# A vision tower on one core: gelu rows weighted before the projection, attention rows divided before P·V, merged products, a new beginning and orders written out

## What is computed

```
h = h + attn0(layernorm(h))     # 16 heads, rope, causal softmax, Wo
h = h + moe(layernorm(h))       # 8 experts, top-2 gates, linear in/out
h = h + attn1(layernorm(h))     # scores, 8 mixed value groups, Wf, relu block
h = h + ffn1(layernorm(h))      # the last stage

def ffn1(x):                    # absmean() makes weights -1, 0 or 1
    h = x @ absmean(W_fc).T     # 256 -> 1024
    h = gelu(h)
    h = (h - mean(h)) * rsqrt(var(h) + eps) * ln_w + ln_b
    return h @ absmean(W_proj).T    # 1024 -> 256
```

## Time and profile before

| | us |
|---|---|
| median of three runs | 561.5 |
| the profiled execution | 560.32 |
| its span | 558.5 |
| TensorE busy | 506.9 (91%) |
| VectorE busy | 375.7 (67%) |
| ScalarE busy | 272.9 (49%) |
| GpSimd busy | 190.3 (34%) |

### The profile page before, as it was taken

One profiled execution on the slowest core, in us unless ns is written; L12 is line 12 of the kernel. 1 busy time (PEld: TensorE's weight loads), 2 busy tenths in 40 slices (PEclk: granted clock), 3 DMA queues, 4 the chain that ended last, 5 costly groups with the idle time before them and its releaser, 6 DMA issues.

```text
span 558.5 us, 12004 instructions
## 1 busy us (share of the span) xinstructions
PE 506.9 (91%) x3850; PEld 424.5 (76%) x3850; DVE 375.7 (67%) x943; ACT 272.9 (49%) x634; POOL 190.3 (34%) x257
## 2 busy tenths in 40 slices
PE   2969999999999887789999999999999989889996
PEld 2758878878787665567778888888888778668885
DVE  4554464555466667565997878878878787648874
ACT  3021213232331363547668777777777886434332
POOL 3320321322323311375463364364363311222230
PEclk9788899999999999999999999999999999979999
DMA  8741333243140500000000000000000000000000
GB/s 318 285 175 38 141 150 120 80 175 150 31 169 0 179 2 2 0 1 2 1 1 2 2 0 0 0 0 0 0 0 0 2 0 1 2 9 21 21 18 22
DMA packets 8685, 29.60 MB, mean 53 GB/s; under 512 B 1936, under 2 KB 3152, under 8 KB 6352
## 3 DMA queue, kind: packets, MB, share of 16 engines
q1 hardware_dynamic: 8656, 29.23, 14.4%
HBM read 27.98 MB, written 1.25 MB: 52 GB/s over the span
## 4 chain that ended last, share of the span: by engine, by line
PE 42%; DVE 5%; issue 5%; ACT 3%; POOL 1%; DVEq 1%; POOLq 0%; ACTq 0%
PE score L2051 6%; PE tb L1803 3%; PE score L1868 3%; PE bz L2081 3%; PE tb L1805 3%; PE tb L1804 3%; PE bank L1805 3%; PE bank L1804 3%; PE bank L1803 3%; PE tb L1886 2%; PE bz L2063 2%; PE bz L1817 2%; PE bz L1803 1%; DVE we_h L1433 1%; PE tb L1817 1%
## 5 line engine op out<-in xcount | busy, mean ns | idle before, releaser
L378 POOL TENSOR_TENSOR h<-h,scaled 114x256 f32 (+1 forms) x88 | 69.0, 784 | 49.3 <-ACT scaled L681 42.7
L330 POOL TENSOR_TENSOR small<-small,half 114x1 f32<-114x1 f32 x44 | 25.7, 584 | 139.4 <-DVE small L964 139.3
L547 ACT ACTIVATE p_exp<-sc,cst 114x608 f32<-114x608 f32 x66 | 48.1, 794 | 24.7 <-DVE sc L1045 24.7
L1915 PE MATMUL bz<-ebuf 128*128 128x256 f32 x256 | 58.9, 383 | 0.0
L1915 PEld LDWEIGHTS bz<-ebuf 128*128 128x128 f32 x256 | 47.8, 192 | 6.0 <-issue 0.2
L1886 PE MATMUL tb<-cst,p_exp 114*114 114x114 f32 x352 | 44.0, 266 | 9.0 <-ACT p_exp L547 3.4
L555 ACT ACTIVATE pt<-tb 114x456 f32<-114x456 f32 x66 | 34.6, 556 | 35.3 <-PE tb L1886 35.3
L2051 PE MATMUL score<-v,pt 114*114 114x137 f32 x352 | 48.9, 282 | 0.3 <-ACT o L648 0.3
L1886 PEld LDWEIGHTS tb<-cst,p_exp 114*114 114x114 f32 x352 | 35.2, 134 | 18.2 <-ACT pt L555 6.7
L681 ACT ACTIVATE scaled<-bank,gl 114x256 f32<-114x256 f32 x88 | 39.0, 473 | 17.3 <-DVE gl L1249 5.9
L2051 PEld LDWEIGHTS score<-v,pt 114*114 114x114 f32 x352 | 44.1, 178 | 2.1 <-issue 0.4
(11 more groups left out here) (216 smaller groups left out, 1338.7 us busy)
## 6 DMA issues: line engine op xcount, KB each, us to landing
ebuf<-in_w_in SPq DMA_DIRECT2D x8, 1024.0 KB, 4.8
ebuf<-in_w_out SPq DMA_DIRECT2D x8, 1024.0 KB, 6.8
x_raw<-in_x_tiles SPq DMA_DIRECT2D x11, 342.0 KB, 3.0
out<-h SPq DMA_DIRECT2D x10, 114.0 KB
raw<-in_w_a SPq DMA_DIRECT2D x4, 256.0 KB, 4.2
ebuf<-in_fc SPq DMA_DIRECT2D x1, 1024.0 KB, 5.6
ebuf<-in_proj SPq DMA_DIRECT2D x1, 1024.0 KB, 7.6
raw<-in_w_a SPq DMA_DIRECT2D x2, 384.0 KB, 5.2
```

What stands on the lines that cost most here:

```text
L378: gp.tensor_tensor(h[0:R, t, :], h[0:R, t, :], scaled[0:R, e % 4, :], ALU.add).then_inc(moe_acc, 1)
L547: act.activation(p_exp[0:R, :, b * S:(b + 1) * S], sc[0:R], ACT.Exp, bias=cst[0:R, CB + b:CB + b + 1], scale=SCALE).then_inc(exps, 1)
L1915: last = pe.matmul(bz[:, m * D:(m + 1) * D], ebuf[:, 0, c * D + m * P:c * D + (m + 1) * P], ebuf[:, 1, c * D:(c + 1) * D], start=(c == 0), ...
```

## The change

**Last stage.** The projection now takes the ternary weights as they are, so two terms suffice. The gelu rows are centred and multiplied by `ln_w` before they are transposed: columns 0 to 511 by GpSimd in two instructions, columns 512 to 1023 by VectorE in one. `proj_hi`, `proj_lo`, `lnw_halves`, `lnw_low`, `proj_sums`, `keep_sums` and `d2_centre` go. The gelu output has two buffers.

```diff
+            def d2_weigh(t):                       # GpSimd
+                gp.wait_ge(g_stat, 4 * t + 4)
+                since(gp, gT_mm, 2 * t)
+                gp.tensor_tensor(gel_w[0:R, 0:512], gel[t % 2][0:R, 0:512], gst[0:R, t, 0:1].broadcast_to([R, 512]),
+                                 ALU.subtract).then_inc(gel_even, 1)
+                gp.wait_ge(gel_even, 2 * t + 1)
+                gp.tensor_tensor(gel_w[0:R, 0:512], gel_w[0:R, 0:512], lnw_row[0:R, 0:512], ALU.mult).then_inc(gel_even, 1)
...
+            def d2_weigh(t):                       # VectorE
+                dve.wait_ge(g_stat, 4 * t + 4)
+                since(dve, gT_mm, 2 * t)
+                V.scalar_tensor_tensor(gel_w[0:R, 512:HID], gel[t % 2][0:R, 512:HID], gst[0:R, t, 0:1], lnw_row[0:R, 512:HID],
+                                       ALU.subtract, ALU.mult).then_inc(gel_odd, 1)
...
             def d2_out(t):
-                V.scalar_tensor_tensor(h[0:R, t, :], x1[0:R], gst[0:R, t, 2:3], h[0:R, t, :],
+                V.scalar_tensor_tensor(h[0:R, t, :], tb[0][0:R, 0:D], gst[0:R, t, 2:3], h[0:R, t, :],
                                        ALU.mult, ALU.add).then_inc(done, 1)
...
             def d2_proj(t):
                 for c in range(HC):
-                    last = mm3(tb[0][0:R, 0:D], gth[:, c, :], gtl[:, c, :], pw_h[c], pw_l[:, c, :], c == 0, c == HC - 1)
+                    pe.matmul(tb[0][0:R, 0:D], gth[:, c, :], projt[:, c, :], start=(c == 0), stop=False)
+                    last = pe.matmul(tb[0][0:R, 0:D], gtl[:, c, :], projt[:, c, :], start=False, stop=(c == HC - 1))
```

**Rows divided.** In the first attention one exponential makes the 608 dense columns, VectorE sums, inverts and multiplies the rows, and three copies scaled by 0 or 1 spread them over the images. The ones products and the division after P·V go; `a2_o` and `a2_lo` read PSUM.

```diff
+            def a2_exp(n):                          # ScalarE
+                act.wait_ge(shifted, 2 * n + 2)
+                act.activation(sc[0:R], sc[0:R], ACT.Exp, scale=SCALE).then_inc(dense, 1)
+
+            def a2_wide(n, batches=range(G)):
+                act.wait_ge(scaled_rows, n + 1)
+                since(act, pt_mm, 4 * n)
+                for b in batches:
+                    act.activation(p_exp[0:R, :, b * S:(b + 1) * S], sc[0:R], ACT.Copy,
+                                   scale=inside[0:R, b:b + 1]).then_inc(exps, 1)
...
+            def a2_norm(n, k):                      # VectorE
+                if k == 0:
+                    V.tensor_reduce(psum_rows[0:R, 0], sc[0:R], AX, ALU.add).then_inc(summed, 1)
+                elif k == 1:
+                    V.reciprocal(psum_rows[0:R, 1], psum_rows[0:R, 0]).then_inc(inverted, 1)
+                else:
+                    V.tensor_tensor(sc[0:R], sc[0:R], psum_rows[0:R, 1].unsqueeze(2).broadcast_to([R, H, S]),
+                                    ALU.mult).then_inc(scaled_rows, 1)
...
             def a_step(t):                          # TensorE
                 scores(t - 1, True)
                 a1_x(t)
                 combine(t, 0)
                 a1_qk(t)
                 a1_v(t)
+                combine(t, 1, (0, 1, 2, 3))
                 a1_turn(t - 1)
-                combine(t, 1)
+                combine(t, 1, (4, 5, 6, 7))
```

```diff
             def c2_qk(t):
-                product(tb[1][0:R, :], xth[1], xtl[1], wc, C_QK, 2 * D, (0, 2 * D)).then_inc(qk1_mm, 1)
+                product(tb[1][0:R, 0:WQ], xth[1], xtl[1], wc, C_QK, W4, (0, WQ)).then_inc(qk1_mm, 1)
             def c2_v(t):
-                product(tb[0][0:R, 2 * R:2 * R + W2], xth[1], xtl[1], wc, C_V, W2, (0, W2)).then_inc(v1_mm, 1)
+                product(tb[0][0:R, 0:D + H], xth[1], xtl[1], wc, C_QK, W4, (WQ, W4)).then_inc(v1_mm, 1)
             def c2_qT(t):
-                pe.wait_ge(qk1_out, t + 1)
+                pe.wait_ge(qk1_out, 2 * t + 2)
+                pe.wait_ge(v1_ready, 2 * t + 2)
```

```diff
+            def warm(n):
+                for i in range(n):
+                    pe.matmul(bz[:, 0:P], ones[:], ones[:], start=True, stop=True)
+
+            pe.wait_ge(init, 2)
+            warm(12)
+            pe.wait_ge(init, 5)
             a1_patch(0)
+            warm(14)
```

More of the change, by code:

```diff
@@ L1783, in _ @@
[L1783 to L1796 removed]
+            d1_x(6)
+            d2_stats(5, (0,))
+            d2_out(2)
+            d2_lo(3, (0, 1))
@@ L1799, in _ @@
+            d2_out(10)
         @block.tensor
@@ L2273, in _ @@
+            c1_x(5)
+            c2_turn_p(2, (2, 3))
             c3_r2(0)
-            with pe.Fori(5, T) as i:
-                c_step(i)
+            c2_x(3)
+            c2_pv(2, (0, 1))
+            c1_gate(5)
+            c3_att(1)
+            c2_pv(2, (2,))
+            c3_wf(1)
+            c2_pv(2, (3,))
+            c2_qk(3)
+            c2_pv(2, (4, 5))
+            c2_v(3)
+            c1_moe(5, (0,))
+            c2_qT(3)
+            c2_kT(3)
+            c3_x(1)
+            c1_x(6)
@@ new lines, in _ @@
+            c2_qT(4)
+            c2_kT(4)
+            c1_x(7)
+            c1_moe(6, (1,))
+            c2_scores(4)
+            c3_x(2)
+            c1_moe(6, (2, 3))
+            c3_r1(2)
+            c2_turn_p(4, (0, 1))
+            c3_r1T(2)
+            c2_turn_p(4, (2, 3))
+            c2_x(5)
+            c1_gate(7)
+            c2_pv(4, (0, 1))
+            c3_r2(2)
+            c2_pv(4, (2,))
+            c3_att(3)
+            c2_qk(5)
+            c2_pv(4, (3, 4))
+            c3_wf(3)
@@ new lines, in _ @@
+            c2_pv(4, (5,))
+            c2_v(5)
+            c1_moe(7, (0,))
+            c2_qT(5)
+            c2_kT(5)
+            c1_moe(7, (1,))
+            c1_x(8)
+            c2_scores(5)
+            c3_x(3)
+            c1_moe(7, (2, 3))
+            c3_r1(3)
+            c2_turn_p(5, (0, 1))
+            c3_r1T(3)
+            c2_turn_p(5, (2, 3))
+            c1_gate(8)
+            c2_x(6)
+            c2_pv(5, (0, 1))
+            c3_r2(3)
+            c2_pv(5, (2,))
+            c2_qk(6)
@@ new lines, in _ @@
+            c3_att(4)
+            c2_pv(5, (3,))
+            c2_v(6)
+            c2_pv(5, (4, 5))
+            c3_wf(4)
+            c2_qT(6)
+            c2_kT(6)
+            c1_moe(8, (0,))
+            c2_scores(6)
+            c1_moe(8, (1, 2, 3))
+            c3_x(4)
+            c2_turn_p(6, (0, 1))
+            c1_x(9)
+            c2_turn_p(6, (2, 3))
+            c2_x(7)
+            c2_pv(6, (0, 1))
+            c3_r1(4)
+            c2_qk(7)
+            c3_r1T(4)
+            c1_gate(9)
@@ new lines, in _ @@
+            c2_pv(6, (2, 3))
+            c2_v(7)
+            c2_pv(6, (4, 5))
+            c3_r2(4)
+            c2_qT(7)
+            c2_kT(7)
+            c3_att(5)
+            c3_wf(5)
+            c2_scores(7)
+            c1_moe(9, (0,))
+            c1_x(10)
+            c1_moe(9, (1,))
+            c3_x(5)
+            c2_turn_p(7, (0, 1))
+            c1_moe(9, (2,))
+            c2_turn_p(7, (2,))
+            c1_moe(9, (3,))
+            c2_turn_p(7, (3,))
+            c2_x(8)
+            c3_r1(5)
@@ new lines, in _ @@
+            c2_pv(7, (0,))
+            c1_gate(10)
+            c2_pv(7, (1, 2))
+            c3_r1T(5)
+            c2_pv(7, (3, 4))
+            c2_qk(8)
+            c2_pv(7, (5,))
+            c2_v(8)
+            c3_r2(5)
+            c2_qT(8)
+            d1_x(0)
+            c2_kT(8)
+            c3_att(6)
+            c3_wf(6)
+            c1_moe(10, (0,))
+            c2_scores(8)
+            c3_x(6)
+            c1_moe(10, (1, 2))
+            c3_r1(6)
+            c2_turn_p(8, (0, 1))
```

1939 lines of the change are left out of this document (1246 added, 693 removed).

## The result

The changed kernel takes **583.04 us** (median of 4 runs, 582.63 to 583.38), the kernel before 561.40 beside it (556.80 to 562.29): ratio 1.040, 95% interval 1.0345 to 1.0459. The forecast was 528 us with a range of 512 to 543 and a chance of 0.95 for faster. It was wrong in its sign. The profiled execution has a span of 581.0 us at a mean granted clock of 0.953 (before 558.5 and 0.977).

The account below looks back on a forecast made before the run. TensorE was taken to set the time nearly everywhere. Savings of 5.5 (beginning), 9.3 (loop), 0.5 (hand-over), 5 (stage C) and 13 (last stage) sum to 33.3 us, giving 528 us; own range 521 to 534, 8 in 10 within 512 to 543.

Parts of the forecast that it names:

- hand-over, 0.5 us earlier, between -3 and +3: From stage A to C: longer softmax waits, about 3 us for each of four tiles, roughly offset by removed work.
- beginning, 5.5 us earlier: Before the loop: warm-up, steadier clock, earlier moments and fewer ones products, less 2.8 us lost as prep_qv waits for prep_products.
- The warm-up: Beginning: idle products raise the clock, saving 1.6 us in the patch product and 1.8 in tile 0's products, 3.4 together.
- Loop: Stage A's loop: ones products and waits before a2_wo and a1_x removed, 1.55 us per pass, 9.3 over six passes.
- the covered chain: Stage A's loop: the softmax chain, 3.1 us longer, hides in 3.8 us of slack, helped by half a combine.
- Rival 2: Hand-over: the clock falls in each of four 3 us waits, about 3.4 us each, 13 in all, 541 us; chance 0.14.
- Stage C, -5: Stage C: merged products and four gate matmuls save 4.3 us, ordered-away idle time 0.7, together 5 us.
- Last stage, -13: Last stage: shorter projection and work moved forward take it from 135.4 to 122 us, 13 saved, between 5 and 20.
- rival 1: Last stage: GpSimd's weighing blocks VectorE at shared ports, 13 us of VectorE, some 8 reaching the end, 536 us; chance 0.17.
- two engines at the same load, and I take 93: Up to c3_r2(10)'s end: TensorE at 83.5 us (59.5 older work plus 24), VectorE at 84, taken as 93.
- The tail: Behind c3_r2(10): 21 us of TensorE, the last tile's 9.5 us chain and the store, taken as 29 us.
- the bare softmax chain: If filler did not cover the chain, eleven tiles wait 3.1 us longer, 34 us, with the clock 575; chance 0.04.

Follow-up runs that it names:

- e1: Changed kernel with ScalarE's tern_sum(0) moved from the head of its list behind the loop to behind a1_pt(8): 573.36 us, ratio 1.026.
- e3: Changed kernel with combine(1, 1) put back ahead of a2_wo(0), prep_qv and a1_patch(2) in TensorE's list: 568.57 us, ratio 1.017.
- e7: e4_both with the division of stage A's rows left out, exponentials with bias going straight to the wide rows: 550.15 us, ratio 0.986.
- e4_both: Changed kernel with both tern_sum(0) moved behind a1_pt(8) and combine(1, 1) put back ahead: 560.91 us, ratio 1.002.
- e6: e4_both with 49 filling products of ones in front of TensorE's waits in the hand-over: 552.20 us, ratio 0.987.
- e17: e4_both with GpSimd's 88 additions of the experts' rows cut to 8 columns in place of 256: 557.93 us, ratio 0.993.
- e18: Kernel before the change with GpSimd's 88 additions of the experts' rows cut to 8 columns in place of 256: 556.87 us, ratio 0.992.
- e9: e4_both with three products per chunk again in d2_proj, the third repeating the low term: 569.16 us, ratio 1.019.
- e10: e4_both with GpSimd's two weighing instructions working on 8 columns in place of 512: 553.12 us, ratio 0.987.

## Why the prediction was wrong

**What failed first: the order of the new steps.** The forecast priced instructions and chains, and took the written-out orders as they came. Its step "hand-over, 0.5 us earlier, between -3 and +3" did not look at what stands at the head of ScalarE's queue and for whose transfer it waits. That omission alone is 10.3 us (e1). Its step "beginning, 5.5 us earlier" named what `prep_qv` waits for, but not that `combine(1, 1)` behind it is what SyncE waits for: 13.7 us (e3, 82.3 to 68.6).

**Beginning.** With that one step put back, 0 to s2 is 10.4 us shorter than before, where 7.0 were forecast with the first pass. The warm-up gives 4 to 6 us, not 3.4: without it the clock also falls again at 35 to 40 us, the stretch that the earlier trace rows shows at 0.71 and whose 3.2 us the forecast had put down to other steps. `prep_qv` waits 2.79 us as forecast (2.8), but only where `combine(1, 1)` stands behind it.

**Loop.** 0.8 us per pass of 1.55. Right: the ones products, the wait before `a2_wo`, and the covered chain (e7 changes the loop by 0.5 us in five passes). Wrong: that VectorE reaches `a1_embed` sooner and so ends the wait before `a1_x`. It stayed at 0.49. And `combine`, cut in two, delays the next load: 0.29.

**Hand-over.** The forecast expected 16 to 17 us without TensorE, and with `tern_sum` moved back there are 17.7 (e4_both). With the clock at 1.00 the stretch takes 74.2 us (e6) where 72.9 were forecast. So apart from `tern_sum` the idle time was right, and what failed is that the term "-3 to +3" had no price for the clock. Rival 2, the falling clock, had a chance of 0.14 and 13 us; it is the cause of 9.2 (e6). The forecast leaned on the waits of 1.7 us that had left the clock at 1.00. In e4_both it fell to its half level within 2.3 us behind four waits, of 1.5, 2.3, 2.3 and 2.8 us. But in the kernel after it stayed at 1.00 through waits of 3.1 and 2.3 us behind c10, and in e6_fill it fell at the same two. The length of a wait alone, then, does not tell what the clock does.

**Stage C, -5.** The products themselves behave as forecast: `c1_gate` has 4 matmuls at 0.10, 392 columns take 0.18, 272 take 0.13. But the stretch from c0 to c9 is 6 us longer instead of shorter, 10.9 over the forecast. 2.1 of it is the lock (e17, e18), the rest are waits and small gaps of open cause.

**Last stage, -13.** The size of the saving was right (e9). Two prices were missing: GpSimd's weighing, at least 6.5 us, rival 1 (0.17), and the tables, 2.6 to 6.4 us, which the forecast does not mention. The guess at the overlap, "two engines at the same load, and I take 93", came out near. Cut as the forecast cut it, the kernel after takes 95.0 us from `c2_x(9)` (450.7) to the end of `c3_r2(10)` (545.7), though the work in it differs by some 1.5 us:
```profile
450.71 0.36 PE L2377 MATMUL tb<-cst,x 114*128 114x114 f32 x2
...
543.83 1.89 PE L2652 MATMUL bz<-wr,x_raw 128*114 128x256 f32 x8
```
The forecast's 59.5 us of older work is not derived from any row. The tail was the worse term: 35.3 us behind `c3_r2(10)` where 29 were forecast, and even on paper 21 us of TensorE, 9.5 of chain and the store are more than 29. There little other work is left to cover a wait: without GpSimd's weighing, r10 to the end falls from 37.2 to 32.5 us (e10).

**The odds.** Slower had 0.04, by one mechanism, the bare softmax chain, which e7 refutes for the loop. What came was the sum of six losses: the two misplaced steps, the clock, GpSimd's weighing, the tables and stage C's gaps. The forecast knew two of them, as rivals that exclude each other. Its range of 15 us to the slow side had room for one stall of 10, not for 56 us.

## What to carry to other kernels

When a written order changes, read the head of each engine's queue at every seam first: what does it wait for, when is that transfer issued, and what stands behind it? Then see what the queue that issues loads waits for, for any product that ends a buffer's use. A wait of TensorE can have a second price, the clock: four waits of 1.5 to 2.8 us here cost 9 us more than their length, which idle products gave back. Other waits of 3.1 and 2.3 us cost nothing of the kind in one execution, so look at the granted clock of each stretch. And in ScalarE's order count the changes between functions, not the calls.
